# Scaling on ScalarE a step ahead of the join, and two groups of TensorE products in the other order, in a graph network of four layers

## The reference

```python
x = layernorm(x + L0(x))            # a graph convolution with sums
x = layernorm(x + L1(x))            # two edge layers, each:
    msg = x[src] @ W_msg + edge_attr @ W_edge
    agg = segment_max(msg, dst); agg = where(isneginf(agg), 0, agg)
    c = leaky_relu(agg + x @ W_root + b)
x = layernorm(x + L2(x))            # softmax-weighted sum of relu(x[src]) + 1e-7 per target
    feats = x + segment_sum(a * m, dst);  L2 = feats @ W + b
x = layernorm(x + L3(x))            # attention with tanh
```

## Time and profile before

| | |
|---|---|
| median of 3 runs | 4280.81 us (4276.13 to 4286.81) |
| profiled execution, its time | 4278.55 us |
| its span | 4276.0 us |
| busy: PE, PEld | 2141.3 us (50%), 1681.9 us (39%) |
| busy: DVE | 2771.2 us (65%) |
| busy: ACT | 1943.7 us (45%) |
| busy: POOL | 2692.4 us (63%) |
| second edge layer | from 2002 to 2551 us |
| third layer | from 2551 to 3228 us |

### The profile page before, as it was taken

How to read it: one execution, slowest core, us unless ns; L and a number is a source line. 1 busy time by engine, 2 the same in 40 slices (tenths; PEclk the granted TensorE clock), 3 DMA queues, 4 the chain that set the end, 5 groups by cost and what they waited for, 6 DMA issues and landing times. The chain is left out here.

```text
span 4276.0 us, 43053 instructions
## 1 busy us (share of the span) xinstructions
PE 2141.3 (50%) x8862; PEld 1681.9 (39%) x8862; DVE 2771.2 (65%) x11287; ACT 1943.7 (45%) x4497; POOL 2692.4 (63%) x2769
## 2 busy tenths in 40 slices
PE   5475445865676677886666646777771000000000
PEld 2121223765565567775444425777771000000000
DVE  8746998337888655664889977777764444444443
ACT  8695000224544322221445544556555555555554
POOL 0277771017777577775777746555536777777776
PEclk9656999555656577776555555556565555555555
DMA  0111221544555466664566645444433222222221
GB/s 6 23 40 39 40 40 48 179 153 130 163 161 154 148 188 201 203 213 154 182 199 205 207 160 161 151 150 159 153 116 87 75 76 77 79 76 76 76 77 50
DMA packets 218624, 521.50 MB, mean 122 GB/s; under 512 B 62234, under 2 KB 69314, under 8 KB 218360
## 3 DMA queue, kind: packets, MB, share of 16 engines
q1 hardware_dynamic: 124040, 363.29, 23.6%
q0 software_dynamic: 94320, 155.47, 16.3%
HBM read 227.56 MB, written 291.01 MB: 121 GB/s over the span
## 5 line engine op out<-in xcount | busy, mean ns | idle before, releaser
L793 POOL DMA_INDIRECT l_G<-y,src x392 | 372.7, 951 | 392.9 <-POOLq L447 273.7
L1370 POOL DMA_INDIRECT l_G<-t,src x392 | 375.4, 958 | 255.0 <-DVE l_inv L1418 123.0
L1903 PE MATMUL l_psR<-l_diag,l_ones 128*128 128x128 f32 x2 | 0.8, 500 | 982.4 <-DVE l_diag L1757 982.4
L1682 POOL DMA_INDIRECT out<-O,nidx x393 | 410.0, 1043 | 127.2 <-issue 124.1
L1667 POOL DMA_INDIRECT l_G<-t,src x392 | 378.7, 966 | 174.2 <-issue 118.3
L1065 POOL DMA_INDIRECT l1a_G<-t,src x392 | 385.6, 984 | 144.6 <-issue 114.3
L1065 POOL DMA_INDIRECT l1b_G<-t,src x392 | 388.5, 991 | 138.9 <-issue 119.2
L532 POOL DMA_INDIRECT O<-x_pad,nidx x393 | 372.9, 949 | 119.7 <-issue 119.7
L1903 PEld LDWEIGHTS l_psR<-l_diag,l_ones 128*128 128x128 f32 x2 | 0.5, 309 | 982.5 <-DVE l_diag L1757 982.5
L117 ACT ACTIVATE O<-O,l_shift,l_rstd 128x96 f32<-128x96 f32 x786 | 292.1, 460 | 167.9 <-DVE l_shift L111 167.9
L929 PE MATMUL l_psP<-l_w,l_xT 97*128 97x192 f32 x786 | 254.5, 513 | 94.3 <-ACT l_xT L889 94.3
(11 more groups left out here) (335 smaller groups left out, 6829.6 us busy)
## 6 DMA issues: line engine op xcount, KB each, us to landing
h<-l_G SPq DMA_DIRECT2D x98, 392.0 KB, 2.4
t<-l1b_t_out SPq DMA_DIRECT2D x49, 768.0 KB, 3.9
h<-l_G SPq DMA_DIRECT2D x49, 768.0 KB
y<-en_y SPq DMA_DIRECT2D x49, 392.0 KB, 2.6
t<-l_t_out SPq DMA_DIRECT2D x49, 392.0 KB, 4.4
l_H<-t SPq DMA_DIRECT2D x49, 392.0 KB, 3.4
en_xT<-x_t SPq DMA_DIRECT2D x49, 384.0 KB, 3.9
t<-l_t_out SPq DMA_DIRECT2D x49, 384.0 KB, 3.8
```

The costliest lines, as they stand in the source:

```text
L793: pool.indirect_dma_start(G[:, s, q, :], None, y0, bass.IndirectOffsetOnAxis(k.src[:, at:at + 1], 0))\
L1370: pool.indirect_dma_start(G[:, s, q, :], None, table, bass.IndirectOffsetOnAxis(k.src[:, at:at + 1], 0))\
L1682: pool.indirect_dma_start(out, bass.IndirectOffsetOnAxis(k.nidx[:, at:at + 1], 0), k.O[:, at, :], None, bounds_check=NP - 1, oob_is_err=Fa ...
```

## The change

In the second edge layer ScalarE gets `mask(c)`: eight Copy activations that multiply the slot's tiles in place by their column of `k.lastok`. It stands after `chain(c+1)`, which still reads the unmasked last row, and after the slot's store. `join(c)` waits for it and adds all eight tiles in one instruction. It moves from step c+1 to c+2, and `factors`, `weigh`, `root`, `apply` and the store of its chunk move by one step too. In VectorE's step `join` and `factors` now stand ahead of `chain`. In the third layer TensorE does `mix` ahead of `multiply`, and `mix` waits for `added`, the end of the addition that reads `N`, in place of `measured`, the end of the statistics.

```diff
@@ -1005,9 +1005,11 @@
             taken_t, taken_r = sem("taken_t"), sem("taken_r")
         else:
             measured, rooted, factored, normed = sem("measured"), sem("rooted"), sem("factored"), sem("normed")
+            masked = sem("masked")
             relued, exped, weighted = sem("relued"), sem("exped"), sem("weighted")
         tile = lambda c: G[:, c % SLOTS, :, :] if c < NCH else F[:, :, :]
-        LAST = NCH + 3
+        LAG = 1 if first else 2
+        LAST = NCH + LAG + 2
         block = ctx.enter_context(nc.Block())
 
         @block.sync
@@ -1048,8 +1050,8 @@
                 if t < NCH:
                     sp.wait_ge(chained, t + 1)
                     sp.dma_start(rows(hist, t), tile(t)).then_inc(kept[t % SLOTS], 16)
-                if t >= 3:
-                    store(t - 3)
+                if t >= LAG + 2:
+                    store(t - LAG - 2)
             for u in range(2):
                 sp.wait_ge(stored[u], (32 if first else 16) * rounds(NCH + 1, u, 2))
 
@@ -1116,7 +1118,10 @@
                 n, s = tiles(c), c % HELD
                 r = R[:, s, 0:n, :]
                 dve.wait_ge(rows_in[s], 16 * (c // HELD + 1))
-                if c < NCH:
+                if not first and c < NCH:
+                    dve.wait_ge(masked, c + 1)
+                    dve.tensor_tensor(r, tile(c), r, ALU.add)
+                elif c < NCH:
                     for q in range(n):
                         at = c * Q + q
                         last = dve.scalar_tensor_tensor(R[:, s, q, :], tile(c)[:, q, :], k.lastok[:, at:at + 1],
@@ -1144,13 +1149,15 @@
                                          ALU.add, ALU.mult).then_inc(weighted, 1)
 
             for t in range(LAST + 1):
+                if not first and 2 <= t < NCH + 3:
+                    join(t - 2)
+                if not first and 3 <= t < NCH + 4:
+                    factors(t - 3)
                 if t < NCH:
                     chain(t)
-                if not first and 2 <= t < NCH + 3:
-                    factors(t - 2)
-                if not first and t >= 3:
-                    weigh(t - 3)
-                if 1 <= t < NCH + 2:
+                if not first and t >= 4:
+                    weigh(t - 4)
+                if first and 1 <= t < NCH + 2:
                     join(t - 1)
                 if t == NCH:
                     close()
@@ -1174,6 +1181,17 @@
                     act.wait_ge(stored[u], 32 * (c // 2))
                 act.activation(t_out[:, u, 0:n, :], P[:, 0:n, 0:D], ACT.Copy).then_inc(taken_t, 1)
                 act.activation(r_out[:, u, 0:n, :], P[:, 0:n, D:2 * D], ACT.Copy).then_inc(taken_r, 1)
+
+            def mask(c):
+                s = c % SLOTS
+                act.wait_ge(chained, min(c + 2, NCH))
+                act.wait_ge(kept[s], 16 * (c // SLOTS + 1))
+                if c == NCH - 1:
+                    act.wait_ge(ends_turned, 1)
+                for q in range(Q):
+                    at = c * Q + q
+                    last = act.activation(tile(c)[:, q, :], tile(c)[:, q, :], ACT.Copy, scale=k.lastok[:, at:at + 1])
+                last.then_inc(masked, 1)
 
             def root(c):
                 u, n = c % 2, tiles(c)
@@ -1202,9 +1220,12 @@
                         take(t - 3)
                     if 2 <= t < NCH + 3:
                         copy(t - 2)
-                elif 2 <= t < NCH + 3:
-                    root(t - 2)
-                    apply(t - 2)
+                else:
+                    if 3 <= t < NCH + 4:
+                        root(t - 3)
+                        apply(t - 3)
+                    if 1 <= t < NCH + 1:
+                        mask(t - 1)
 
         @block.tensor
         def _(pe):
@@ -1323,6 +1344,7 @@
         turned_v = sem("turned_v")
         copied_v = sem("copied_v")
         mixed = sem("mixed")
+        added = sem("added")
         measured = sem("measured")
         rooted = sem("rooted")
         factored = sem("factored")
@@ -1424,7 +1446,7 @@
             def measure(c):
                 u, n = c % 2, tiles(c)
                 dve.wait_ge(mixed, c + 1)
-                dve.tensor_tensor(k.O[:, cols(c), :], k.O[:, cols(c), :], N[:, 0:n, 0:D], ALU.add)
+                dve.tensor_tensor(k.O[:, cols(c), :], k.O[:, cols(c), :], N[:, 0:n, 0:D], ALU.add).then_inc(added, 1)
                 dve.drain()
                 norm_stats(dve, lambda q: k.O[:, c * Q + q, :], n, st, mv, u, measured)
 
@@ -1530,7 +1552,7 @@
             def mix(c):
                 pe.wait_ge(copied_v, c + 1)
                 if c >= 1:
-                    pe.wait_ge(measured, c)
+                    pe.wait_ge(added, c)
                 for q in range(tiles(c)):
                     last = pe.matmul(N[:, q, 0:D], vT[:, q * 128:(q + 1) * 128], wg[:, :], start=True, stop=True)
                 last.then_inc(mixed, 1)
@@ -1558,10 +1580,10 @@
                     pe.matmul(sums, k.carry_from[:, :], tile(NCH - 1)[:, Q - 1, :], start=True, stop=True)\
                       .then_inc(carried, 1)
                     pe.wait_ge(copied, 1)
+                if 2 <= t < NCH + 3:
+                    mix(t - 2)
                 if 5 <= t < NCH + 6:
                     multiply(t - 5)
-                if 2 <= t < NCH + 3:
-                    mix(t - 2)
                 if 4 <= t < NCH + 5:
                     turn_x(t - 4)
                 if 1 <= t < NCH + 2:
```

## The result

The changed kernel takes 4311.59 us (median of 5 runs, 4302.21 to 4315.04) against 4284.48 for the kernel before in the same series: 1.0062 times as long, with a 95% interval of 1.0046 to 1.0079. That is 27 us more. The forecast was 4318 us, which was 37 more than the 4280.8 us of the kernel before that it started from.

A forecast was written before the change was run, and what follows sets the result against it. Bounds taken: VectorE and gathers in the second edge layer (10.40 us a step), a TensorE-ScalarE circle in the third (12.86). 4280.8 + 145 loss - 108 gain = 4318 us, slower by 0.9%; range 4288 to 4372.

The forecast's parts named there:

- The circle in the second edge layer: Second edge layer: closed chain of waits from `join` through ScalarE's mask to the next `join`, 13.36 us a step against 10.40.
- statistics, apply and mask follow one another: Second edge layer: sentence saying these three now run in sequence, where apply ran beside the next join before.
- the walk just above it: Second edge layer: link-by-link sum of one step, from `join(t-2)` at 0 to `join(t-1)` at 13.36 us.
- The stage's loss: Second edge layer: 145 us lost, 133 of them as 45 * 2.96, the rest the longer tail.
- The third layer's gain: Third layer: `mix` first shortens TensorE's gap from 2.79 to 1.10 us; step 12.86 to 10.5, gain 108 us.
- rival 2: Third layer: clock holds at full, step falls to VectorE's 10.05 us, gain 129, total 4297 us; chance 0.15.
- the prediction's own formula: Third layer: share of TensorE's work at full clock, (10.55 - work per step)/4.8; 28% needed, 10% before.
- the next bound: Third layer: VectorE's own 10.0 us or the gathers, together 10.05 to 10.4 us a step.
- the 10.3 to 10.8 us that the profile was to show: Third layer: expected distance between chains in the profile after; over 11.5 us a step would refute the prediction.
- Rival 1: Third layer: TensorE's clock does not rise, step 11.17 to 11.65 us, gain 57 to 78, total 4348 to 4369; chance 0.25.
- The neighbours' queues: Second edge layer: SP's loads, GpSimd's gathers and the stores were claimed to add nothing to the loss.
- The tail: Second edge layer: work after `join(47)` at about 2662, ending at about 2693.

The follow-up runs named there:

- e4: Changed kernel with VectorE doing `weigh(t-4)` ahead of `chain(t)`, on the slower chip: 5396.69 us, 0.9764 of the kernel before.
- f3: Changed kernel with ScalarE's mask between the eight activations of `apply` and its Relu, repeat run on the slower chip: 5451.97 us, 0.9867 of the kernel before.
- f9: As f3, with VectorE's statistics of `join(t-2)` moved behind `chain(t)`, on the slower chip: 5387.61 us, 0.9741 of the kernel before.
- e5: Changed kernel without ScalarE's mask: `join` does its eight multiply-adds again, still a step later: 4160.91 us, 0.9724 of the kernel before.
- e6: Kernel before with the third layer's new order, `mix` still waiting for `measured`: 4162.62 us, 0.9724 of the kernel before.
- e7: Kernel before with only the wait changed to `added`, old order of the products: 4275.98 us, 0.9992 of the kernel before.
- e1: Kernel before with the third layer's new order and wait on `added`, second edge layer unchanged, on the slower chip: 5415.39 us, 0.9800 of the kernel before.
- f: Group of kernels on the slower chip, repeating those with e and the same number, plus the new f9; kernel before there: 5526 and 5531 us.
- f4: Repeat of e4, changed kernel with `weigh(t-4)` ahead of `chain(t)`, on the slower chip: 5391.58 us, 0.9743 of the kernel before.
- f1: Repeat of e1, third layer's new order and wait alone against the kernel before, on the slower chip: 5427.98 us, 0.9823.
- e8: Kernel before with the third layer's new order and wait on `added`, `mix` also waiting for `copy_x`: 4274.37 us, 0.9989 of the kernel before.

## Why the prediction was right, point by point

**The circle in the second edge layer** had the right links, and its size within 0.1 us: 13.36 forecast, 13.40 in most steps and 13.46 as the mean. The signal from the mask to the addition is 0.11 us where 0.03 was assumed, which the shorter mask (2.21 for 2.24) and other small terms offset to 0.04; the rest of the mean are the few steps in which the chain stood still. Only the sentence "statistics, apply and mask follow one another" names a path that isn't the longest: by the walk just above it `weigh` ends later (9.28) than `apply` (8.40), and so it is in the trace. e4 moves `weigh` out of the way and the step loses 0.96 us. f3 takes out Relu with its wait, and Exp, and comes to 10.8 against 10.7 in undisturbed steps. f9 opens the circle. e5 takes out the mask with its arrow, and the loss is gone. The stage's loss of 149.6 against 145 is 0.1 us in 45 steps.

The Trainium skill's figure (ScalarE: Activation LUTs, Rules for kernel authors) gave an estimate of 3.0 us for eight scalings without overlap; eight in a row take 2.21 us here. What made the mask dear was its place in the queue.

**The third layer's gain** had the right mechanism, and one term too small: the step was taken as 10.5 us and is 10.19, 43 * 0.31 = 13 us of the 14 missing. The step was taken above its floor because TensorE's clock was expected to rise only partly. It did rise only partly, to 0.70 in the steady part, and not to the full clock of rival 2. But that was enough to reach the floor. TensorE's work is 320.99 us in 390 us, 8.4 a step, where 9.2 would have fitted and before had 10.07; by the prediction's own formula that is (10.55 - 8.4)/4.8 = 45% of the work at full clock, where 28% were enough. What bounds the step now is GpSimd's gathers (10.17 us for eight), which the prediction had named together with VectorE as the next bound at 10.05 to 10.4. So 10.5 us kept a margin above the bound that nothing filled. In step length the result lies nearer to rival 2 (10.05) than to the forecast, and just below the 10.3 to 10.8 us that the profile was to show. Rival 1, the clock that stays low, did not happen; its evidence, 10.55 us without a rise, was one stretch.

**The rest.** The neighbours' queues added nothing, as worked out: GpSimd's new wait of 3.7 us a step is a consequence and not a cause. `added` was costed at nothing, and e6 and e7 measure nothing. The tail came as forecast: from `join(47)` to the last operation 30.8 us (2662.15 to 2692.99), forecast 31. Of the 11.5 us by which the end behind the last chain grew (38.9 against 27.4), e5 shows 4.8 with the later `join` alone. The two errors, 5 us of loss and 14 of gain, have opposite signs in the sum and leave 37 - 9 = 28 against 27 measured. That the total came out within 10 us is in part owed to this.

**A version that beats both:** the second edge layer as before with TensorE's new order, 4162.62 us with the old wait, and 4160.91 with `added` and the later join: 2.8% under the kernel before. Only the half of the change that shortens a wait pays.

## What to carry to other kernels

Moving work to an engine with idle time is judged by the order of its queue, not by its busy share: draw for one step who waits for whom, and add up each closed chain. Here ScalarE went from 47% to 51% busy in the stage and the step grew by 3 us, because the moved piece stood behind work that itself waits for the receiver. Where such a chain exists, put the moved piece ahead of the work that nobody in the chain waits for. In TensorE's queue, let first come what needs the earliest copy, so that the other copies run under its products.

## What the runs showed of the hardware that was not expected

**Engines that stand still on one chip.** On the chip of e1 to e4 and f, the same instructions have the same lengths, and the idle time before some groups of them has grown. VectorE's aggregations in the kernel before, and in e1 on that chip (busy us, mean ns, idle us and what ended it):

```profile
L106 DVE BATCH_NORM_AGGREGATE l_mv<-l_st 128x2 f32<-128x6 f32 x1179 | 96.2, 153 | 12.2 <-issue 0.7
```

```profile
L106 DVE BATCH_NORM_AGGREGATE l_mv<-l_st 128x2 f32<-128x6 f32 x1179 | 96.2, 153 | 162.4 <-issue 153.8
```

96.2 us and 153 ns in both, but 162.4 us idle ahead in place of 12.2, of which 153.8 with nothing that the trace shows to wait for. It isn't every group: these are the aggregations of the layers other than the edge layers, and those of the second edge layer have 3.6 us of idleness before and 3.7 in e1, while the chain there goes from 46.4 to 188.5. What holds the instructions back is not shown. A kernel whose engines idle in every step seems to hide these holes: f4 keeps 12.4 us in all but a few steps, while the edge layer of before goes 10.2, 17, 10.2, 17. So the closed circle of 12.4 us was the faster one there, 0.9743 for f4 against 0.9823 for f1. On the other chip, where a step of before has 10.40 us, f4 was not run.

**TensorE's clock with a short gap in every step.** With a gap of 1.1 us ahead of `mix` the clock changes between its two levels (1.2 and 2.4 GHz) from one step to another, 0.70 in the mean of 2760 to 3150 us. With gaps of 2.8 us it was 0.59 over the third layer of before, and in e8, with the gap back in the new order, 0.61 between 2800 and 2900 us.
